# Cross-attention on one core: how the q and k stacks of a batch are laid out, loaded and stored

## What is computed

```python
q = split_heads(x @ w_q)
k, v = split_heads(text @ w_k), split_heads(text @ w_v)
out_text = merge_heads(sdpa(q, k, v))
k_ip, v_ip = split_heads(ip_h @ w_k_ip), split_heads(ip_h @ w_v_ip)
out_ip = merge_heads(sdpa(q, k_ip, v_ip, mask=mask_ip))
return (out_text + out_ip) @ w_out + b_out + x
```

## Time and profile before

| | us |
|---|---|
| median of 3 runs | 677.06 (675.39 to 678.09) |
| the profiled execution: its own time | 672.22 |
| its span, first to last instruction | 670.2 |
| PE busy | 521.4 (78%) |
| DVE busy | 385.0 (57%) |
| ACT busy | 279.1 (42%) |
| POOL busy | 126.6 (19%) |
| DMA | 107.87 MB, mean 161 GB/s |
| mean granted TensorE clock | 0.883 of full speed |

### The profile page before, as it was taken

How to read it: one execution, slowest core, us unless ns; L and a number is a source line. 1 busy time by engine, 2 the same in 40 slices (tenths; PEclk the granted TensorE clock), 3 DMA queues, 4 the chain that set the end, 5 groups by cost and what they waited for, 6 DMA issues and landing times.

```text
span 670.2 us, 12777 instructions
## 1 busy us (share of the span) xinstructions
PE 521.4 (78%) x4304; PEld 342.6 (51%) x4304; DVE 385.0 (57%) x706; ACT 279.1 (42%) x355; POOL 126.6 (19%) x203
## 2 busy tenths in 40 slices
PE   4988898998990767398698698586985986968986
PEld 3866677776860634154354354353552543534543
DVE  2583422423331356387677688574983875848852
ACT  3441333334230024255454555443652553635571
POOL 4040000000000001222221321321331321322231
PEclk9989899899896686697978989887997888969998
DMA  9987677767769947687577767866786775776211
GB/s 274 274 169 219 216 243 259 230 212 268 231 204 160 209 125 159 86 165 155 85 169 147 106 170 145 109 168 109 147 159 92 162 152 83 161 153 98 85 44 39
DMA packets 90878, 107.87 MB, mean 161 GB/s; under 512 B 14890, under 2 KB 69878, under 8 KB 90826
## 3 DMA queue, kind: packets, MB, share of 16 engines
q1 hardware_dynamic: 90074, 106.11, 67.8%
q0 software_dynamic: 752, 1.07, 1.4%
HBM read 68.99 MB, written 38.17 MB: 160 GB/s over the span
## 4 chain that ended last, share of the span: by engine, by line
DMA 33%; PE 24%; SPq 14%; issue 12%; DVE 10%; ACT 4%; POOL 2%; ACTq 0%; DVEq 0%; POOLq 0%
PE pv L746 11%; DMA max_rows<-row_buf 8%; DMA k_stack<-k_parts 7%; DMA q_parts<-qk_out 5%; DMA stack<-k_parts 5%; DMA v_rows<-v_out 5%; PE score_t L732 4%; SPq L290 3%; SPq L214 3%; PE score_q L682 3%; SPq L219 3%; DVE max_cols L550 2%; ACT probs L487 2%; DMA probs<-in_wv_ip 2%; PE pj L755 2%
## 5 line engine op out<-in xcount | busy, mean ns | idle before, releaser
L550 DVE TENSOR_REDUCE max_cols<-score_q 128x4 fp32r<-128x992 f32 x160 | 187.1, 1169 | 133.0 <-PE score_q L682 132.3
L487 ACT ACTIVATE probs<-score_t 128x1024 f32<-128x1024 f32 x160 | 163.5, 1022 | 75.6 <-PE score_t L732 74.2
L746 PE MATMUL pv<-probs,v_cur 128*32 128x256 f32 x1920 | 141.5, 435 | 1.8 <-DMA v_cur<-v_sp_rows 1.2
L478 ACT ACTIVATE o_all<-pv 128x512 f32<-128x512 f32 x80 | 47.9, 599 | 132.8 <-PE pv L746 132.8
L403 POOL TENSOR_TENSOR o_turned<-o_turned,inv_cols 128x256 f32<-128x256 f32 x80 | 49.6, 620 | 253.9 <-DVE inv_cols L605 253.8
L682 PE MATMUL score_q<-k_stack,q_stack 53*128 53x256 f32 x440 | 51.0, 313 | 51.1 <-DMA k_stack<-k_parts 42.9
L746 PEld LDWEIGHTS pv<-probs,v_cur 128*32 128x32 f32 x1920 | 59.6, 121 | 51.2 <-issue 19.3
L732 PE MATMUL score_t<-q_stack,k_stack 55*128 55x256 f32 x440 | 59.5, 351 | 26.3 <-ACT probs L487 17.3
L732 PEld LDWEIGHTS score_t<-q_stack,k_stack 55*128 55x128 f32 x440 | 36.1, 202 | 74.6 <-ACT probs L487 34.2
L755 PE MATMUL pj<-wo_sb,o_all 128*128 128x320 f32 x192 | 70.2, 476 | 2.7 <-DVE o_all L610 1.9
L397 POOL TENSOR_TENSOR x_all<-x_all,bias_sb 128x640 f32<-128x640 f32 x16 | 24.8, 1548 | 232.8 <-DMA x_all<-in_x 232.6
(11 more groups left out here) (132 smaller groups left out, 722.9 us busy)
## 6 DMA issues: line engine op xcount, KB each, us to landing
k_stack<-k_parts SPq DMA_DIRECT2D x66, 160.0 KB
v_rows<-v_out SPq DMA_DIRECT2D x32, 320.0 KB, 3.1
v_cur<-v_rows SPq DMA_DIRECT2D x16, 640.0 KB
o_all<-in_ctxT SPq DMA_DIRECT2D x16, 512.0 KB, 6.6
q_parts<-qk_out SPq DMA_DIRECT2D x32, 256.0 KB
k_parts<-qk_out SPq DMA_DIRECT2D x32, 248.0 KB
q_stack<-q_parts SPq DMA_DIRECT2D x22, 320.0 KB
x_all<-in_x SPq DMA_DIRECT2D x16, 320.0 KB, 5.1
```

Source lines behind the costliest of these rows:

```text
L478: nc.scalar.activation(o_raw[:, k, :], pv[:, :], ACT.Copy)\
L487: nc.scalar.activation(probs[:, slot(u, p), :], score_t[:, :], ACT.Exp, scale=SCALE)\
L550: nc.vector.tensor_reduce(out=max_cols[:, h, :, at:at + 2].rearrange("p t e -> p e t"), in_=both[:, :, :, 0:TEXT], op=ALU.max, axis=AX.X, ...
L746: last = mm(pv[32 * t:32 * t + 32, at:at + S], values_of(u, kind, 4 * k + t), probs[:, slot(u, 2 * k + t // 2), a:a + S], start=kind != 1, ...
```

## The change

A stack's rows are laid out otherwise. Kinds are now four (three of q or k rows, the fourth holds masks, maxima and zeros), and they are interleaved: kind j sits on partitions j, j+4, j+8 and so on, 32 of them, over all 128. So a kind is one transfer of 32 rows by ten blocks of 256 (320 KB), and a stack is 7 transfers: three of q, one of the fourth kind, three of k. The matmuls over a stack take 64 rows. The fourth kind comes from `aux_rows`, now 32 rows for a batch, whose 11 unused rows for each half of the heads are zeroed once by two transfers from a new buffer `zeros`; its loads grow from 100 KB to 320 KB for a stack. `kaux_rows` grows in the same way, and its loads are one transfer a stack instead of two. A half of the maxima goes in with one transfer instead of two.

`q_parts` is laid out as [2, 320, 4096], as `k_parts` was.

In a batch, SP issues the output's store and the residual first, then the 7 transfers in a row with no wait between them, then values and maxima. The waits after 4, 6, 7 and 8 pairs are gone.

```diff
-    q_parts = nc.dram_tensor("q_parts", [H, 2, DH, B * S], f32, kind="Internal").ap()
+    q_parts = nc.dram_tensor("q_parts", [2, D, B * S], f32, kind="Internal").ap()
...
+        def rows_of(stack, kind):
+            return stack[kind::KINDS, :].rearrange("p (a n) -> p a n", a=PAIRS).bitcast(f32)
...
-                        sp.dma_start(q_parts[8 * m:8 * m + r // DH, s, :, bass.ds(g * GT, GT)], src[:, s, :])\
+                        sp.dma_start(q_parts[s, m * P:m * P + r, bass.ds(g * GT, GT)], src[:, s, :])\
...
             def load_rows(t, h):
                 sp.wait_ge(rows_stored, 16 * (2 * t.b + h + 1))
-                for e in range(2):
-                    at = HEAD * e + PART + MASKS
-                    sp.dma_start(
-                        q_stacks[t.w][at:at + 2, h * HALF * S:(h + 1) * HALF * S].rearrange(
-                            "p (a n) -> p a n", a=HALF).bitcast(f32),
-                        max_rows[h][0:4 * HALF, :].rearrange("(a k e) n -> e k a n", k=2, e=2)[e])\
-                        .then_inc(rows_loaded[h], 16)
+                dst = q_stacks[t.w][2 * DH - 1::2 * DH, h * HALF * S:(h + 1) * HALF * S]
+                sp.dma_start(dst.rearrange("p (a n) -> p a n", a=HALF).bitcast(f32),
+                             max_rows[h][0:4 * HALF, :].rearrange("(a x) n -> x a n", x=4)).then_inc(rows_loaded[h], 16)
...
-            def load_q(t, e):
-                at, done = HEAD * e, stack_loaded[t.w]
...
-                sp.dma_start(qv[at:at + DH, :, :], cols[e, 0:DH]).then_inc(done, 16)
-                sp.dma_start(qv[at + DH:at + PART, :, :], cols[e]).then_inc(done, 16)
...
+            def load_q(t, j):
+                src = q_parts[j // 2, :, bass.ds(t.b * S, S)].rearrange("(a er) n -> er a n", a=PAIRS)
+                sp.dma_start(rows_of(q_stacks[t.w], j), src).then_inc(stack_loaded[t.w], 16)
+            def load_aux(t):
+                src = aux_rows[bass.ds(t.b, 1), :, :].rearrange("a r n -> (a r) n")
+                sp.dma_start(rows_of(q_stacks[t.w], KINDS - 1),
+                             src.unsqueeze(1).broadcast_to([2 * DH, PAIRS, S])).then_inc(stack_loaded[t.w], 16)
             def load_k(t, j):
...
-                for e in range(2):
-                    at = HEAD * e + DH * j
-                    sp.dma_start(kv[at:at + DH, :, :], src[e]).then_inc(stack_loaded[t.w], 16)
+                src = k_parts[j % 2, :, bass.ds(t.b * KEYS, KEYS)].rearrange("(a er) n -> er a n", a=PAIRS)
+                sp.dma_start(rows_of(k_stacks[t.w], j), src).then_inc(stack_loaded[t.w], 16)
...
                 if not first:
                     load_rows(t, 1)
-                scored(t, 0)
-                if ahead:
-                    load_q(t.to(2), 0)
                 if t.there(-2):
                     store_out(b - 2)
                 load_residual(b, u)
+                if ahead:
+                    scored(t, 0)
+                    load_stack(t.to(2))
                 if next_:
                     need(sp, pv_ready, QUADS * b)
                     load_values(b + 1, 1 - u)
-                scored(t, 4)
-                if ahead:
-                    load_q(t.to(2), 1)
-                if next_:
                     store_rows(b + 1, 0)
-                scored(t, 6)
-                if ahead:
-                    load_k(t.to(2), 0)
-                if next_:
                     load_rows(t.to(1), 0)
-                for j in (1, 2):
-                    if ahead:
-                        scored(t, 6 + j)
-                        load_k(t.to(2), j)
-                if next_:
                     store_rows(b + 1, 1)
...
+            aux_of = aux_rows.rearrange("b (e r) n -> b e r n", e=2)
+            for e in range(2):
+                pool.dma_start(aux_of[:, e, MASKS:DH, :], zeros[:, :].unsqueeze(1).broadcast_to(
+                    [B, DH - MASKS, S])).then_inc(aux_stored, 16)
```

86 lines of the change are left out of this document (40 added, 46 removed).

## The result

| | before | after |
|---|---|---|
| median, both run in turn on one chip | 676.22 (673.76 to 678.09) | 557.89 (554.59 to 559.58) |
| the profiled execution: its own time | 672.22 | 556.40 |
| its span | 670.2 | 554.6 |
| mean granted TensorE clock | 0.883 | 0.972 |

The ratio is 0.825, with a 95% interval of 0.819 to 0.830: the change takes 118 us away. Four executions each stand behind the medians. The prediction said 568, with 550 to 600 around it.

The account below looks back on a forecast made before the run. Waits were taken to bound the kernel: PE's for k loads (66.8 us), ACT's for q stores (57.5). 672.2 + 2 - 18 - 13 - 4 - 75 = 564.2 us for the profiled execution, 568 as a median, range 550 to 600.

Parts of the forecast that it names:

- Group stage: Groups 1 to 6: q stores run on 16 engines, so the period falls from 24.3 to 21.3 us, gaining 18 us.
- The rival of the value stores taking over: Group stage: waits for value stores replace those for q stores and the period stays; median 586 us, chance 0.08.
- Stack rate: Stack loads: interleaved rows move at 265 GB/s, between 128 and 353, so a stack takes 8.5 us.
- engines meeting: Stack loads: engines working on like rows at the same moment hold the rate near 200 GB/s; median 597 us, chance 0.2.
- The expected sign: Windows of stack loads in the new profile: 265 GB/s at a share near 1.
- the rival of the full rate: Stack loads: rows spread over all partitions move at 353 GB/s, like the values; median 555 us, chance 0.2.
- Batch stage: Batches 1 to 14: a two-batch loop through the maxima sets a period of 20.5 us against 25.86, gaining 75 us.
- Last group: Last group: faster stack loads let the value store land 24.1 us after the first load, not 36.7, gaining 13 us.
- Batch 0: End of batch 0: its 5.12 us wait for maxima shrinks, gaining 4 us, bounds 0 to 5.
- Small parts: Start and matmuls: zeros and larger constants lose 2 us at the start; matmuls over 64 rows cost nothing.
- The one in which loads stay slow: Stack loads: they stay at 128 GB/s in the new layout; median 649 us, chance 0.04.
- The slower one: Batches: the burst holds up the maxima, the period exceeding 25.86 once a stack takes over 19.2 us; median 701, chance 0.03.

Follow-up runs that it names:

- maxima ahead: The kernel after, with store and load of the first half of the maxima issued ahead of the next batch's values: 543.22 us, ratio 0.809.
- the order-only kernel: The kernel before with SP's new order alone, its old layout and twelve transfers a stack: 695.15 us against 675.41, ratio 1.033.

## Why the prediction was right, step by step

**The view of the kernel before** held. What was named as the waits (k loads, q stores) is what went, and the 19.9 us of ten pairs with nothing late is the floor that maxima ahead comes down to (20.02).

**Group stage: right, the size a little low.** Predicted a period of 21.3 and 18 us; measured 20.9 (groups 2 to 6; group 1 took 23.2 where it took 26.7) and 20.3. A row of the chain after, and a group's window, one period long:

```profile
171.57 2.33 DMA q_parts<-qk_out
```

```profile
128.80:149.70 20.90, 20.90 (x110) 17.24 (x109) 8.23 (x10) 8.67 (x13) 0.00 (x0) 1.00 0.82 274
```

PE is busy for all of the 20.90 us, so it sets the period, as the sum over its matmuls (21.0) said. The store that was expected at 3.5 us on the chain is 2.33. The rival of the value stores taking over fell: PE waits for none of them there.

**Stack rate: the number nearly right, the reason wrong.** 265 GB/s was a choice between two ends, with engines meeting as the reason. Windows of the kernel after: the wait for the first stack, the burst in each of two batches, and 2 us of stack loads alone:

```profile
181.00:186.00 5.00, 0.00 (x0) 0.00 (x0) 0.00 (x0) 0.37 (x1) 0.00 (x0) 0.93 1.01 336
```

```profile
406.50:419.00 12.50, 12.20 (x138) 7.35 (x138) 11.89 (x25) 7.66 (x10) 4.76 (x7) 1.00 0.82 261
...
386.50:399.00 12.50, 12.00 (x138) 6.80 (x133) 12.21 (x27) 7.60 (x10) 4.81 (x8) 1.00 0.89 291
...
412.00:414.00 2.00, 2.00 (x22) 0.97 (x14) 1.76 (x5) 1.25 (x3) 1.87 (x2) 1.00 1.01 344
```

Where the engines are full the rate is near that of the values, 336 and 344 GB/s at a share of 1.01. So engines don't meet in a way that shows. A burst, which has output, residual and values in it too, comes to less, since its share is below 1: fourteen windows of this length, one for each burst, run from 261 to 295 GB/s with 291 in the middle, and the first of the two above is the lowest. The share is low while SP still issues: 0.79 at 255 GB/s in the first 6 us of a burst (470 to 476), then 1.02 at 348 (476 to 482). The expected sign, 265 GB/s at a share near 1, was therefore wrong in its second half, and the rival of the full rate had the hardware right. What neither counted is SP's time. The issues of one batch in the kernel after:

```profile
466.07 0.53 SPq L227 DMA_DIRECT2D max_rows<-row_buf  x1
468.94 0.54 SPq L232 DMA_DIRECT2D q_stack<-max_rows  x1
469.59 0.42 SPq L336 DMA_DIRECT2D out<-out_sb  x1
...
470.86 2.19 SPq L278 DMA_DIRECT2D stack<-q_parts  x3
473.23 0.60 SPq L281 DMA_DIRECT2D stack<-aux_rows  x1
473.92 1.99 SPq L285 DMA_DIRECT2D stack<-k_parts  x3
...
477.20 0.60 SPq L227 DMA_DIRECT2D max_rows<-row_buf  x1
483.55 0.57 SPq L232 DMA_DIRECT2D q_stack<-max_rows  x1
```

The seven transfers hold SP from 470.86 to 475.91, 5.1 us, at 0.60 to 0.73 each; over the batches it is 4.8 to 6.5, the longest where SP was held once for some two us more (the two burst windows above are of the batches with 6.2 and 6.5). That is less than the 6.5 us that the stack's bytes take at 350 GB/s, so SP costs a burst about a fifth of its first 6 us, and does not set the whole of its length.

**Batch stage: right.** The loop is seen in these rows as the prediction laid it out. From the second maxima's store (466.07, its 0) the maxima land and their load is issued at 2.9 (predicted 2.9), the output at 3.5 (3.4), the first stack transfer at 4.8, the first maxima's store at 11.1; that lands at 17.5 (17.9), and PE starts pair 0 at 485.71, which is 19.6 (19.8). Over thirteen rounds the landing is at 16.5 to 19.5, 17.4 in the middle. The wait of PE at 485.71 is 1.13 us, and there are eight such waits at the 15 turns (seven in the row above, one on `stack`), about every second one, as was expected. The mean period is 20.82 where 20.5 was predicted and 19.9 stands for the full rate. The term was 75 us and measured 70.6. The 0.3 of a period that is missing isn't in the loop's middle round, which by the same sum gives 20.4; the rounds scatter (19.7 to 22.6 us), and one that follows the longest wait (3.24 us, at 276.00) took 22.3 at a granted clock of 0.85. The experiments bear the loop out from both sides: fewer bytes ahead of the maxima, 20.0; more, 21.9, by half of their own time.

**Last group: 16.8 us for 13, on another path than the one summed.** The issues of the kernel after there:

```profile
169.94 3.58 SPq L218 DMA_DIRECT2D q_parts<-qk_out  x6
173.93 2.09 SPq L278 DMA_DIRECT2D q_stack<-q_parts  x3
...
182.40 3.47 SPq L285 DMA_DIRECT2D k_stack<-k_parts  x3
185.91 4.58 SPq L223 DMA_DIRECT2D k_parts<-qk_out  x6
190.53 7.73 SPq L246 DMA_DIRECT2D v_rows<-v_out  x4
```

The k stores are issued 12.0 us after the first stack load, where it was 21.4, and the value store in question landed 23.4 us after that load (24.1 predicted, 36.7 before). PE waits 5.12 us for the stack where it waited 19.55. But the value store is no longer what the first key scores wait for. The chain after has no store of values on it there; it comes from batch 0's stack:

```profile
178.05 7.92 DMA k_stack<-k_parts
```

From its landing (PE starts at 186.01, 12.1 us after the first load) it runs through PE and DVE to 211.75. These 25.7 us, at a granted clock of 0.81, are the work that the prediction put at about 17 and set aside. From the first stack load to the first key scores it is 37.8 us, where it was 49.2: a gain of 11.4, less than the 13. The other 5.4 lie ahead of that load, and the prediction had no term for them: the load waits for the q stores of the group before, and goes out 3.3 us after the group's first k matmul (173.93) where it took 8.7 (199.74). That the sum at 353 GB/s would have given 17 is chance.

**Batch 0: 6.4 us for 4.** It still ends with a wait for maxima, but of 2.04 us and not 5.12. It was bounded at 5, the wait that was there. Without their waits the batch took 23.3 us before and 20.0 after, at a mean granted clock of 0.70 and 0.84, for which the sum had no term.

**Small parts.** The 2 us more at the start did not come: the first k matmul of group 1 is at 42.73, as before. POOL's stores and the larger constants are hidden. Matmuls over 64 rows cost nothing that shows: the period comes down to that of before's undisturbed pairs.

**The rivals.** Engines meeting (597) and the group stage keeping its period (586) were wrong. Full rate (555) was right on the packets, and nearest in time, but its period of 19.9 wasn't reached; the maxima still waited behind the burst, as the run with maxima ahead shows by reaching it. The one in which loads stay slow (649) is near the order-only kernel: that has 695, and with the 18 us of the q stores, which it lacks, 677, so this rival was priced some 28 us too low. The slower one (701) had this mechanism, but put its turning point at a stack of over 19 us; a period of 27.0, where it saw the gain of the groups used up (27.1), came already with the burst at some 160 GB/s (158 from its start to the landing of the maxima), the values in it slowed too. Together they had 0.07, and it was the layout that kept them away.

The total is 7.8 us too high against the profiled execution (564.2 against 556.4), and that it came so near owes something to errors of opposite sign. Gain was counted too low by 2.3 in the groups, 3.8 in the last group, 2.4 in batch 0, 2.1 at the start and 1.4 at the end, and too high by 4.4 in the batches.

## What to carry to other kernels

Ask of a row's layout in SBUF which partitions a transfer writes: the same 1 KB packets took 145 ns to 16 adjoining partitions (403 to 406, before) and 48 to rows spread over all. A small transfer that somebody waits for should be issued ahead of the bulk on its queue, not behind it, and every store and load of such a round trip counts; here moving them ahead of the values was worth 2.3% after a change that had already brought 17%. And two halves of a change should be tried apart: the order, which does no harm on top of the layout, cost 3% alone.
